# A two-layer graph kernel on one core: the node stage reads its inputs from PSUM with the bias added by a matmul and GpSimd's addition first, and the aggregation is unrolled with a destination factor for every tile

## What is computed

```python
deg = segment_sum(ones_like(dst), dst)              # self loops included
dinv = rsqrt(deg)
norm = dinv[src] * dinv[dst]
H = X @ W
out = segment_sum(H[src] * norm[:, None], dst) + b  # self loops included
x1 = layernorm(X + where(out >= 0, out, 0.01 * out))
```

## Time and profile before

| | |
|---|---|
| median of 3 runs | 1660.66 us (1659.83 to 1660.71) |
| the profiled execution | 1665.52 us, of which its span is 1663.4 us |
| VectorE busy over the span | 1235.9 us (74%) |
| GpSimd busy over the span | 1111.2 us (67%) |
| TensorE busy over the span | 1390.4 us (84%), 7928 matmuls |
| mean granted TensorE clock | 0.961 of full speed |

### The profile page before, as it was taken

How to read it: one execution, slowest core, us unless ns; L and a number is a source line. 1 busy time by engine, 2 the same in 40 slices (tenths; PEclk the granted TensorE clock), 3 DMA queues, 4 the chain that set the end, 5 groups by cost and what they waited for, 6 DMA issues and landing times. The chain is left out here.

```text
span 1663.4 us, 26922 instructions
## 1 busy us (share of the span) xinstructions
PE 1390.4 (84%) x7928; PEld 1140.6 (69%) x7928; DVE 1235.9 (74%) x2017; ACT 553.6 (33%) x996; POOL 1111.2 (67%) x1146
## 2 busy tenths in 40 slices
PE   1888895888888839999999999999999934767766
PEld 1888894666666629999999999999999832333332
DVE  4545544999999952778788888788888775766666
ACT  1555551444444421322222232222322111333333
POOL 3766625777777733467767777777777556777775
PEclk9999997999999969999999999999999966999999
DMA  4778644666666632334554334553344424776775
GB/s 126 221 237 265 217 176 148 190 189 189 189 189 189 190 105 86 111 107 133 149 165 114 114 127 126 146 172 114 114 127 125 121 71 127 255 235 235 233 239 185
DMA packets 123981, 272.39 MB, mean 164 GB/s; under 512 B 19504, under 2 KB 19952, under 8 KB 123808
## 3 DMA queue, kind: packets, MB, share of 16 engines
q1 hardware_dynamic: 93472, 176.89, 32.8%
q0 software_dynamic: 29920, 93.89, 19.0%
q10 hardware_dynamic: 544, 1.05, 0.2%
HBM read 198.22 MB, written 73.61 MB: 163 GB/s over the span
## 5 line engine op out<-in xcount | busy, mean ns | idle before, releaser
L159 PE MATMUL pse<-w_lo,w_hi 128*128 128x256 f32 (+1 forms) x1440 | 466.2, 324 | 24.6 <-DVE w_lo L1051 21.1
L161 PE MATMUL pse<-w_hi 128*128 128x256 f32 (+1 forms) x1440 | 461.8, 321 | 0.0
L160 PE MATMUL pse<-w_hi,w_lo 128*128 128x256 f32 (+1 forms) x1440 | 461.8, 321 | 0.0
L159 PEld LDWEIGHTS pse<-w_lo,w_hi 128*128 128x128 f32 x1440 | 277.0, 192 | 44.9 <-issue 23.7
L161 PEld LDWEIGHTS pse<-w_hi 128*128 128x128 f32 x1440 | 276.7, 192 | 19.8
L160 PEld LDWEIGHTS pse<-w_hi,w_lo 128*128 128x128 f32 x1440 | 277.2, 193 | 18.7
L895 POOL TENSOR_TENSOR acc_x<-acc_x,node_rows 128x512 f32<-128x512 f32 (+1 forms) x79 | 129.9, 1644 | 94.3 <-DMA node_rows<-x_table 89.6
L1291 PE MATMUL psf<-fin_x,ident 128*128 128x512 f32 x158 | 88.1, 640 | 70.2 <-POOL fin_x L1261 65.5
L159 PE MATMUL psn<-w_lo,agg_hi 128*128 128x512 f32 x316 | 133.8, 423 | 2.9 <-DVE agg_lo L713 2.9
L160 PE MATMUL psn<-w_hi,agg_lo 128*128 128x512 f32 x316 | 126.6, 401 | 0.0
L161 PE MATMUL psn<-w_hi,agg_hi 128*128 128x512 f32 x316 | 126.5, 400 | 0.0
(11 more groups left out here) (191 smaller groups left out, 3287.0 us busy)
## 6 DMA issues: line engine op xcount, KB each, us to landing
coef_all<-coef_table SPq DMA_DIRECT2D x40, 512.0 KB
node_x<-in_x SPq DMA_DIRECT2D x79, 256.0 KB
x_table<-node_x SPq DMA_DIRECT2D x79, 256.0 KB, 2.1
node_rows<-x_table SPq DMA_DIRECT2D x79, 256.0 KB
fin_x<-x_table SPq DMA_DIRECT2D x79, 256.0 KB
out_dram<-fin_y SPq DMA_DIRECT2D x78, 256.0 KB, 2.1
edge_part<-part SPq DMA_DIRECT2D x20, 512.0 KB
sum_table<-sums SPq DMA_DIRECT2D x40, 256.0 KB
```

The costliest lines, as they stand in the source:

```text
L159: pe.matmul(to, left[0], right[1], start=first, stop=False)
L160: pe.matmul(to, left[1], right[0], start=False, stop=False)
L161: return pe.matmul(to, left[0], right[0], start=False, stop=last)
```

## The change

In the aggregation, GpSimd's index copy is gone and its loop is written out for all 40 tiles, so that the gathers read their indices in `edge_idx` itself. A fourth gather fetches dinv of the destination, for every tile, into `dinv_dst`, which is kept for the whole stage. ScalarE multiplies by it as it copies the sums out of PSUM. So `sum_table` holds sums that are already scaled by the destination's dinv, G uses dinv squared, and the product comes out with both factors in it.

In the node stage the bias is a thirteenth matmul of 512 columns in each tile's group: a square of ones times a tile whose first two rows are the bias's high and low part. Z becomes a plain copy by ScalarE from PSUM to `node_z`, and L reads the product from PSUM and `node_z` from SBUF. G is one VectorE instruction for every tile. GpSimd's loop is written out, its index copy and its share of G are gone, and Y stands ahead of the gather. Rings of y and x1 have 4 places in place of 2, the pipeline is two iterations longer (9 in place of 7), and V is a `tensor_scalar` with two per-partition scalars.

```diff
@@ index_stage (edge_idx has 5 columns in place of 4)
+                v.scalar_tensor_tensor(g.edge_idx[:, :, 4], low[:, 0, :], float(NT), high[:, 0, :], ALU.mult, ALU.add)
...
+                dve.wait_ge(dinv_ok, 1)
+                v.tensor_tensor(g.dinv_sq[:], g.dinv[:], g.dinv[:], ALU.mult)
@@ aggregate_stage
-                def step(t, s, on):
+                def rows_of(table, to, t, i):
+                    at = bass.IndirectOffsetOnAxis(ap=g.edge_idx[:, t, i:i + 1], axis=0)
+                    return nc.gpsimd.indirect_dma_start(out=to, out_offset=None, in_=table, in_offset=at)
+                for t in range(ET):
+                    s = t % R
                     wait(pool, ea_t, t - R + 1)
+                    rows_of(g.ea, ea_rows[:, s, :], t, 0).then_inc(ea_in[s], 16)
                     wait(pool, scaled_ok, t - R + 1)
-                    nc.gpsimd.tensor_copy(idx[:, s, :], g.edge_idx[:, bass.ds(t, 1), 0:3].rearrange("p t c -> p (t c)")).then_inc(idx_ok, 1)
-                    wait_alone(pool, idx_ok, t + 1, g.passed)
-                    for i, (to, of, n) in enumerate(((ea_rows, g.ea, ea_in), (x_rows, g.x, x_in), (dinv_src, g.dinv_table, x_in))):
-                        nc.gpsimd.indirect_dma_start(...)
-                sweep(pool, ET, 0, R, R, step)
+                    rows_of(g.x, x_rows[:, s, :], t, 1).then_inc(x_in[s], 16)
+                    rows_of(g.dinv_table, dinv_src[:, s, :], t, 2).then_inc(x_in[s], 16)
+                    rows_of(g.dinv_table, dinv_dst[:, t, :], t, 4).then_inc(x_in[s], 16)
...
-                            act.wait_ge(x_in[2 * s + q], 2 * landed(j, s, 0, 2))
+                            act.wait_ge(x_in[2 * s + q], 3 * landed(j, s, 0, 2))
...
-                            nc.scalar.copy(sums[:, q, :], ps_back[q][:]).then_inc(row_ok, 1)
+                            nc.scalar.activation(sums[:, q, :], ps_back[q][:], ACT.Copy, scale=dinv_dst[...]).then_inc(row_ok, 1)
@@ node_stage, GpSimd
+                for j in range(NT + 7):
+                    if j >= 7:
+                        i = j - 7
+                        pool.wait_ge(leaky_ok, i + 1)
+                        wait(pool, x1_ok, i - RY + 1)
+                        nc.gpsimd.tensor_tensor(y[:, i % RY, :], z[:, i % 2, :], xr[:, i % RX, :], ALU.add).then_inc(y_ok, 1)
+                    if j < NT:
+                        wait(pool, agg_ok, j - RS + 1)
+                        nc.gpsimd.indirect_dma_start(out=rn[:, j % RS, :], out_offset=None, in_=g.sum_table,
+                                                     in_offset=bass.IndirectOffsetOnAxis(ap=g.last_edge[:, j:j + 1], axis=0)).then_inc(rn_in[j % RS], 16)
@@ node_stage, ScalarE
+                    if on(6):
+                        act.wait_ge(mm_ok, j - 5)
+                        wait(act, y_ok, j - 7)
+                        nc.scalar.copy(z[:, q, :], ps_o[(s - 6) % 4][:]).then_inc(z_ok, 1)
+                    if on(3):
+                        act.wait_ge(turned, j - 2)
+                        nc.scalar.copy(g_hi[:, h, :, :], by_k(ps_t[h][:])).then_inc(hi_ok, 1)
+                    if on(9):
+                        act.wait_ge(scale_ok, 2 * (j - 9) + 2)
+                        nc.scalar.activation(x1[:, q, :], y[:, q, :], ACT.Identity, bias=mv[:, h, 3:4], scale=mv[:, h, 2:3]).then_inc(x1_ok, 1)
+                    if on(8):
+                        act.wait_ge(stat_ok, 2 * (j - 8) + 2)
+                        nc.scalar.activation(root[:, h, :], mv[:, h, 1:2], ACT.Sqrt, bias=g.eps[:]).then_inc(root_ok, 1)
@@ node_stage, VectorE
+                    if on(6):
+                        dve.wait_ge(z_ok, j - 5)
+                        v.scalar_tensor_tensor(z[:, q, :], ps_o[(s - 6) % 4][:], NEG_SLOPE, z[:, q, :], ALU.mult, ALU.max).then_inc(leaky_ok, 1)
+                    if on(3):
+                        dve.wait_ge(hi_ok, j - 2)
+                        v.tensor_tensor(g_lo[:, h, :, :], by_k(ps_t[h][:]), g_hi[:, h, :, :].bitcast(F32), ALU.subtract).then_inc(lo_ok, 1)
...
+                        v.scalar_tensor_tensor(gr[:, h, :], xr[:, (s - 2) % RX, :], g.dinv_sq[:, bass.ds(j - 2, 1)], rn[:, (s - 2) % RS, :], ALU.mult, ALU.add).then_inc(agg_ok, 1)
@@ node_stage, TensorE (its product is two iterations behind the transposes, before one)
+                        pe.matmul(to, ones_r[:], b_two[:], start=True, stop=False)
```

More of the change, by code:

```diff
@@ L579, in node_stage @@
         RS = 4
-        idx = sb(ctx, "node_idx", [P, RS, 1], I32)
+        RY = 4
         xr = sb(ctx, "node_x", [P, RX, D])
@@ L601, in node_stage, with by_k @@
             "node_z_ok", "node_leaky", "node_y_ok", "node_stat", "node_root_ok", "node_scale", "x1_ok"))
-        x1_out = [sem(f"x1_out{s}") for s in range(2)]
+        x1_out = [sem(f"x1_out{s}") for s in range(RY)]
         def by_k(row):
             return row.rearrange("p (k e) -> p k e", k=K)
[L607 to L612, removed]
+        def by_k(row):
+            return row.rearrange("p (k e) -> p k e", k=K)
         with nc.Block() as block:
@@ L683, in _ @@
                 dve.wait_ge(b_in, 48)
-                def step(j, s, on):
-                    h = s % 2
-                    if on(2) and h == 0:
+                v.tensor_copy(ones_r[:], g.ones[:])
+                v.tensor_copy(b_hi[:], b_row[:]).then_inc(b_ok, 1)
+                dve.wait_ge(b_ok, 1)
+                v.tensor_tensor(b_row[:], b_row[:], b_hi[:].bitcast(F32), ALU.subtract).then_inc(b_ok, 1)
+                v.tensor_scalar(z[:, 0, :], b_hi[:].bitcast(F32), g.ident[:, 0:1], None, ALU.mult).then_inc(b_ok, 1)
+                dve.wait_ge(b_ok, 3)
+                v.scalar_tensor_tensor(b_two[:], b_row[:], g.ident[:, 1:2], z[:, 0, :], ALU.mult, ALU.add).then_inc(b_ok, 1)
+                def step(j, s, on):
+                    if on(6):
+                        q = (s - 6) % 2
+                        dve.wait_ge(z_ok, j - 5)
+                        v.scalar_tensor_tensor(z[:, q, :], ps_o[(s - 6) % 4][:], NEG_SLOPE, z[:, q, :], ALU.mult, ALU.max).then_inc(leaky_ok, 1)
+                    if on(3):
+                        h = (s - 3) % 2
+                        dve.wait_ge(hi_ok, j - 2)
+                        v.tensor_tensor(g_lo[:, h, :, :], by_k(ps_t[h][:]), g_hi[:, h, :, :].bitcast(F32), ALU.subtract).then_inc(lo_ok, 1)
+                    if on(8):
+                        m = (s - 8) % 2
+                        dve.wait_ge(y_ok, j - 7)
+                        v.bn_stats(stats[:, m, :], y[:, (s - 8) % RY, :]).then_inc(stat_ok, 1)
+                    if on(9):
+                        m9 = (s - 9) % 2
+                        dve.wait_ge(root_ok, j - 8)
+                        v.reciprocal(mv[:, m9, 2:3], root[:, m9, :]).then_inc(scale_ok, 1)
+                    if on(8):
+                        wait(dve, x1_ok, j - 9)
+                        wait_alone(dve, stat_ok, 2 * (j - 8) + 1, g.passed)
+                        v.bn_aggr(mv[:, m, 0:2], stats[:, m, :]).then_inc(stat_ok, 1)
+                    if on(9):
+                        dve.wait_ge(scale_ok, 2 * (j - 9) + 1)
+                        v.tensor_scalar(mv[:, m9, 3:4], mv[:, m9, 0:1], mv[:, m9, 2:3], -1.0, ALU.mult, ALU.mult).then_inc(scale_ok, 1)
+                    if on(2):
+                        h = s % 2
                         dve.wait_ge(x_in[(s - 2) % RX], landed(j, s, 2, RX))
```

118 lines of the change are left out of this document (38 added, 80 removed).

## The result

The changed kernel takes 1954.82 us (median of 4 runs, 1942.33 to 1966.5), the kernel before 1660.68 beside it. The ratio is 1.1759, with a 95% interval of 1.1677 to 1.1841. The forecast was 1652 us and a 0.69 chance of faster; the kernel is 294 us slower.

The account below looks back on a forecast made before the run. It took VectorE's order to bound the node stage, with producer and TensorE nearly level in the aggregation. Node stage -16, aggregation +7 and index tables +0.4 sum to -8.6: 1652 us from the median 1660.7, range 1636 to 1667.

Parts of the forecast that it names:

- the second loop of the node stage: Node stage: G, transposes, H, then O, running beside the 3.95 us loop; O could start at 3.77.
- H may start at 3.13 (0.48 behind Z): Node stage: H follows the transposes, which end at 3.06, and Z on ScalarE; it ends at 3.72.
- It has 0.18 to spare: Node stage: the loop through G, transposes and H lets O start at 3.77, against 3.95 us a tile.
- +2: Node stage: cost in us of the pipeline being two iterations longer, with bounds 0 and 2 x 3.95.
- the six cases: Whole kernel: the forecast itself, 1652 us at chance 0.45, and five rivals with their own times and chances.
- Case 2: Node stage: TensorE's 3.53 us a tile binds, not the order; 1620 us, halfway 1636; chance 0.10.
- The first loop: Node stage: O, S, A, V, X1, root, Z, L, O sets the pace, 3.95 us a tile against 4.17.
- +7 forecast: Aggregation: net cost in us, from 1.6 + 6.6 less 1.0 for the first gather without a copy.
- TensorE's 4.98: Aggregation: TensorE's pace in us a tile, from edge-row transposes over 39 tiles; the producer's 5.02 would exceed it.
- the bound of +21: Aggregation: upper bound in us, if all of the 0.50 us a tile to spare is delay of gathers themselves.
- the fifth case: Aggregation: it pays in full, +20 us, giving 1665 us; chance 0.10.

Follow-up runs that it names:

- run 18: The changed kernel with the product one iteration behind the transposes in place of two, on the fifth chip: 1653.19 us, ratio 0.9989.
- the sixth run: The kernel before with GpSimd's three aggregation gathers written out and the index copy gone, no fourth gather: 1637.55 us, ratio 0.9889.
- run 11: The changed kernel with the product one iteration behind the transposes and X1 one iteration later on ScalarE: 1719.78 us, ratio 1.0305.

## Why the prediction was wrong

**The step that failed** is the second loop of the node stage: "H may start at 3.13 (0.48 behind Z)" and "It has 0.18 to spare". H was given two conditions, the transposes and its place behind Z. It has a third, `mm_ok` of the tile two back, which the text never priced, although the header of TensorE's part in the diff says that the product is two iterations behind; the line with that wait was left out of the quoted diff too. The forecast took the deeper pipeline for a cost at the stage's end only ("+2"). The runs put 7.71 us in place of 3.95 for a tile: 3.76 x 78 = 293 us, of a miss of 301 in the profiled run (1958.2 against 1657). Of these an estimate from the two kinds of turn above, (6.92 - 3.95) x 78, gives some 230 us to the chain at full clock and the other 60 to the lower clock. None of the six cases held it. Case 2, in which TensorE would set the pace, was judged by its 3.53 us of work and not by the order of its queue.

**The first loop was right.** O, S, A, V, X1, root, Z, L, O: forecast 3.95, measured 3.91, 3.92 and, by G's rows of the last run, 3.93, once the product's place is mended. One turn of run 18:

```profile
431.69 0.68 DVE L704 TENSOR_TENSOR agg_lo<-psn,agg_hi 128x512 fp32r<-128x512 f32 x1
...
432.28 0.68 DVE L709 BATCH_NORM_STATS2 node_stats<-node_y 128x6 f32<-128x512 f32 x1
...
433.12 0.18 DVE L718 BATCH_NORM_AGGREGATE node_mv<-node_stats 128x2 f32<-128x6 f32 x1
433.21 0.18 DVE L721 TENSOR_SCALAR node_mv<-node_mv 128x1 f32<-128x1 f32 x1
...
433.51 0.82 ACT L676 ACTIVATE node_x<-node_y,node_mv 128x512 f32<-128x512 f32 x1 [1.89 <-DVE node_mv L721]
...
434.23 0.28 ACT L680 ACTIVATE node_root<-node_mv,eps 128x1 f32<-128x1 f32 x1
434.41 0.56 ACT L664 COPY node_z<-psn 128x512 f32<-128x512 f32 x1
...
435.01 0.69 DVE L700 SCALAR_TENSOR_TENSOR node_z<-psn,node_z 128x512 f32<-128x512 f32 x1 [0.87 <-ACT node_z L664]
...
435.62 0.68 DVE L704 TENSOR_TENSOR agg_lo<-psn,agg_hi 128x512 fp32r<-128x512 f32 x1
```

By starts, with the forecast in brackets: O to S 0.59 (0.58), S to A 0.84 (0.85), A to V 0.09 (0.09), V to X1 0.30 (0.21), X1 to root 0.72 (0.72), root to Z 0.18 (0.20), Z to L 0.60 (0.64), L to O 0.61 (0.66): 3.93 (3.95). X1 waits for V and L for Z, and the others follow their queue, as written. The trace shows this chain; no run took a link out of it without bringing in another wait.

**The durations of the node stage** held. In the changed kernel L takes 0.69 at its median (0.74 forecast), G 0.75 (0.74), V 0.18 (0.16), and Z 0.56 (0.59). G is never held.

**The aggregation** hit its sum with its parts wrong, and that was luck. The transposes ended 5.2, 6.9 and 8.8 us later than in the earlier trace rows where there were no stalls (+7 forecast), and the gathers are 1.25 apart. But "TensorE's 4.98" was not TensorE's: in the sixth run it takes (198.0 - 38.0) / 39 = 4.1 us a tile. And the profile of the earlier trace rows has 13.4 us of stalls in it, which the prediction read as TensorE's pace. Without them its transposes would have ended near 219 by an estimate. Two others are near it: 225.9 less 5.9 of stalls on chip 4, 220, and 198.0 + 16.3 on chip 2, where the whole of the sixth is 16.3 us under the kernel before, 214. Measured from there, writing three gathers out gains 16 to 22 us, the fourth costs 41 (198.0 to 239.0, both on chip 2), and the two together cost 17 to 27. That is the bound of +21 and the fifth case, put at 0.10.

**What was not foreseen at all**: the stalls, up to 62 us for the same kernel by chip; and the two last stages, whose code is the same. From the first load of `edge_part` on they took 1042.9 us in the profile before, 1049.9 in the changed one, and 1042.3 to 1051.4 over all twenty profiles; the cause stays open. Together with a before that ran 1652.80 on the last chip and not 1660.7, this is why the mended change, whose profiled span of 1654.5 is 8.9 under that of the first profile of before, comes out at 0.9989. Its node stage has what was forecast (G over 306.2 us in place of 324.9, 18.7 less), so by the whole time the other stages cost as much again on that chip, which an aggregation of +17 to +27 would account for; the kernel before has no profile there.

## What to carry to other kernels

- When an edit changes the distance between pipeline steps, write out each in-order queue for three neighbouring tiles, and under every instruction all of its waits, those for a free ring place too. A ring of two is enough only while the reader of tile i - 2 stands ahead of the producer's input of tile i in the queue.
- If all engines become idle together, look in the list of waits for the one that ends on the *last* instruction of a long group. Here H waiting for L162 named the fault at once, and one iteration of distance gave back some 294 us.
- Compare variants on one chip, and run the first surprise again on another: a side effect that follows the chip looks like one of the program as long as each chip has seen only one kind.

## What the hardware did that was not expected

- TensorE's pauses. On chips 1, 3 and 4 it stopped between matmuls of the aggregation for up to 3.1 us at a time (run 11); on chips 2 and 5 and in the first run of the changed kernel never. On chip 4 the kernel before had 5.9 us of it in the aggregation, the changed kernel 49; the first profile of before had 13.4. The Trainium skill, Runtime: NRT & Kernel Launch, section "Instruction fetch mechanics", says that engines fetch their instructions by DMA in the background, mostly hidden, and that full unrolling is to be preferred to branches. That the pauses are late instructions is not shown, and the traces speak against it: between 40 and 235 us on chip 4 the changed kernel had 50 pauses (37 us), while the DMA queues moved 5 packets of kind "instruction", against 7 in its first profile, which has no pause. Nor was unrolling a gain there: with GpSimd's loop written out and its copy gone the transposes ended 13 us later (239.2 against 225.9), while on chip 2 the same edit made the whole kernel 1.1% faster. What the pauses are, and why chips differ in them, stays open.
- The granted clock fell with the serial pace. In the changed kernel's node stage it is 0.86 on the mean, between the two levels of 1.2 and 2.4 GHz, and 0.99 in the mended one with TensorE busy 261 of 285 us. An order that leaves TensorE idle pays twice: 6.92 us for a turn at full clock, and 8.46 for the same turn where the granted clock was near 0.80.
- A gather of 128 elements of 4 bytes holds GpSimd's queue as long as one of 128 rows of 512 features: 0.95 us and 0.30 to the next, against 0.97 and 0.30. Four gathers take 5.02 us a tile where TensorE needs 4.1, and that is 36 of the 41 us that the fourth cost.
